# Composite step weights on four row groups, high parts by GpSimd, copies by ScalarE, ahead of a recurrent block

## What is computed

```
x  += cross_attention(x, ctx, mask)          # 16 heads of 8
x  += windowed_attention_with_sinks(x)       # 16 heads of 64, rotary
x  += moe(x)                                 # 8 experts of 512, top 2, and a shared one
x  += attention_lstm(layernorm(x), ctx)      # 32 steps, one after the other
x   = four mamba layers, two halves of the batch
x  += low-rank gated feed-forward(x)
```

## Time and profile before

| what | value |
|---|---|
| three runs | 659.81, 659.59, 658.29 us; median 659.59 |
| profiled execution | 659.47 us, of which the span from first to last instruction is 657.7 us |
| busy share of the span | PE 84%, DVE 72%, ACT 47%, POOL 27% |
| chain of work that ended last | PE 40%, DVE 29%, ACT 13%, issue 11%, POOL 5% |
| prologue of the recurrence | about 200 to 212 us after the span's start |
| recurrence | about 212 to 433 us |

### The profile page before, as it was taken

The page is one execution under the profiler, slowest core; times in us unless marked ns, Lnnn a source line. Parts: engine busy times, 40 slices in busy tenths (PEclk is TensorE's granted clock), DMA queues, the critical chain, the costliest instruction groups (busy, mean ns, idle before and its releaser), DMA issues.

```text
span 657.7 us, 20735 instructions
## 1 busy us (share of the span) xinstructions
PE 553.9 (84%) x8471; PEld 424.7 (65%) x8471; DVE 471.3 (72%) x1834; ACT 306.5 (47%) x902; POOL 179.3 (27%) x217
## 2 busy tenths in 40 slices
PE   6968778669997999999999999966998898889856
PEld 4535543358875888888888888854655665666544
DVE  2978638875345677777777777752898899899883
ACT  3768636226556344434443444335545554555501
POOL 4255629227000000000000000005357346634700
PEclk9979969699995555555555555557988998899887
DMA  9900000010002000000000000000000000000000
GB/s 315 421 8 2 1 5 0 2 47 1 1 5 92 4 4 3 4 4 3 4 4 4 4 3 4 5 2 0 1 0 1 1 1 0 1 1 0 1 0 9
DMA packets 6256, 16.07 MB, mean 24 GB/s; under 512 B 2656, under 2 KB 3432, under 8 KB 5648
## 3 DMA queue, kind: packets, MB, share of 16 engines
q1 hardware_dynamic: 5744, 14.47, 6.0%
q10 hardware_dynamic: 416, 0.26, 0.1%
HBM read 14.60 MB, written 0.13 MB: 22 GB/s over the span
## 4 chain that ended last, share of the span: by engine, by line
PE 40%; DVE 29%; ACT 13%; issue 11%; POOL 5%; DMA 1%; DVEq 0%; ACTq 0%; POOLq 0%
PE bank L1721 8%; PE bank L1627 6%; PE bank L1789 6%; ACT esp L666 3%; PE bank L1557 3%; PE bank L1570 2%; DVE ssum L1168 2%; ACT a L653 2%; ACT e L668 2%; DVE asp L1158 2%; DVE rz L1203 2%; DVE opre L1144 2%; POOL T L438 2%; DVE opre L1147 2%; DVE opre L1145 2%
## 5 line engine op out<-in xcount | busy, mean ns | idle before, releaser
L1627 PE MATMUL bank<-esp,qblk 128*128 128x1 f16 (+1 forms) x2048 | 66.8, 167 | 11.9 <-ACT esp L666 11.9
L474 POOL MEMSET ctxT<- 128x128 f32 x1 | 0.3, 312 | 277.7 <-DVE xres L1210 277.7
L1627 PEld LDWEIGHTS bank<-esp,qblk 128*128 128x128 f16 x2048 | 61.4, 104 | 17.2 <-ACT esp L666 17.2
L1627 PE MATMUL bank<-hsp,kT 128*128 128x2 f16 x2048 | 63.5, 166 | 1.9 <-DVE hsp L1196 1.7
L1627 PEld LDWEIGHTS bank<-hsp,kT 128*128 128x128 f16 x2048 | 59.5, 104 | 2.0 <-issue 1.9
L653 ACT ACTIVATE a<-opre 128x4 f32<-128x4 f32 x64 | 13.1, 205 | 80.8 <-DVE opre L1147 80.8
L1236 DVE SCALAR_TENSOR_TENSOR T<-bank,bct,T 128x256 f32<-128x256 f32 x112 | 46.4, 473 | 2.2 <-PE bank L1802 2.2
L1223 DVE TENSOR_TENSOR_SCAN qblk<-ctxT,bank 128x512 f32<-128x512 f32 x32 | 37.7, 1208 | 5.6 <-PE bank L1789 5.3
L660 ACT ACTIVATE gact<-bank,lgate 128x16 f32<-128x16 f32 x64 | 17.5, 274 | 46.3 <-PE bank L1627 46.3
L1223 DVE TENSOR_TENSOR_SCAN w<-kT,bank 128x512 f32<-128x512 f32 x32 | 37.6, 1205 | 1.1 <-PE bank L1789 1.1
L1627 PEld LDWEIGHTS bank<-asp,lsp 128*128 128x128 f16 x768 | 25.5, 105 | 17.2 <-DVE asp L1158 17.1
(11 more groups left out here) (331 smaller groups left out, 1411.6 us busy)
## 6 DMA issues: line engine op xcount, KB each, us to landing
w<-in_w_dram SPq DMA_DIRECT2D x2, 2048.0 KB
ctxT<-in_ctxT_dram SPq DMA_DIRECT2D x8, 256.0 KB, 6.7
wqkv<-in_qkvT_dram SPq DMA_DIRECT2D x1, 1536.0 KB, 12.2
w<-in_mw_dram SPq DMA_DIRECT2D x1, 1024.0 KB, 4.9
lw<-in_lw_dram SPq DMA_DIRECT2D x1, 960.0 KB, 23.6
rows<-in_rows_dram SPq DMA_DIRECT2D x1, 772.0 KB, 9.9
wqkv<-in_fw_dram SPq DMA_DIRECT2D x1, 532.0 KB, 3.6
T<-in_mask_dram SPq DMA_DIRECT2D x1, 512.0 KB, 5.9
```

The lines of the kernel that those rows point to most:

```text
L1627: return pe.matmul(out, lhsT, rhs, start=start, stop=stop, skip_group_check=True)
```

## The change

The composites of the four layers move to the four row groups of the array: layer l has its two factors on partitions 32l to 32l+7. `dtw` comes in four transfers instead of one. The eight small turns become matmuls with the identity that write 32 rows each (8 useful), so that layer l's rows come out on partitions 32l; ACT copies them in four pieces. In the prologue the composites' matmuls go through the layers for the first chunk and then for the second, and wait first for two gates' outputs on ACT. ACT writes only `gx32`; POOL rounds it to the high part; DVE keeps its three operations on each gate and loses the composites' copies, which ACT takes over after its table load. `l_gxps` and `m_comp` become one semaphore, `l_ps`.

```diff
-        m_dt = maskb[:, :].bitcast(F32)[:, 0:ML * MC * MR]
+        m_dt = maskb[:, :].bitcast(F32)[:, 0:ML * MC * MR + 32]
-        dtw = maskb[0:MR, :].bitcast(F32)[:, 1024:1024 + ML * MI]
-        xpd = wqkv[0:MR, 1856:1856 + ML * MI]
+        dtw = [maskb[32 * l:32 * l + MR, :].bitcast(F32)[:, 1024:1024 + MI] for l in range(ML)]
+        xpd = [wqkv[32 * l:32 * l + MR, 1856:1856 + MI] for l in range(ML)]
...
-            sp.dma_start(dtw, arr["dtw"]).then_inc(sem["d_ssm"], 16)
+            for l in range(ML):
+                sp.dma_start(dtw[l], arr["dtw"][:, l * MI:(l + 1) * MI]).then_inc(sem["d_ssm"], 16)
...
+            for g in range(4):
+                pool.wait_ge(sem["l_gx"], g + 1)
+                pool.tensor_scalar(gx[:, 0:S, 0, g, :], gx32[:, :, g * B:(g + 1) * B], 1.0, 0.0, ALU.mult, ALU.add) \
+                    .then_inc(sem["l_gxhigh"], 1)
...
-            for k in range(2):
-                act.activation(xpd[:, k * 512:(k + 1) * 512], bank[2 + k][0:MR, :], ACT.Copy).then_inc(sem["m_wdt"], 1)
+            for l in range(ML):
+                act.activation(xpd[l], bank[2][32 * l:32 * l + MR, 0:MI], ACT.Copy).then_inc(sem["m_wdt"], 1)
...
-                act.wait_ge(sem["l_gxps"], g + 1)
+                act.wait_ge(sem["l_ps"], g + 1)
-                for to in (gx32[:, 0:1, g * B:(g + 1) * B], gx[:, 0:1, 0, g, :]):
-                    ins = act.activation(to_time(to), share, ACT.Identity, bias=gbias[:, g:g + 1],
-                                         scale=lgx[:, g // 3:g // 3 + 1])
-                ins.then_inc(sem["l_gx"], 1)
+                act.activation(to_time(gx32[:, 0:1, g * B:(g + 1) * B]), share, ACT.Identity, bias=gbias[:, g:g + 1],
+                               scale=lgx[:, g // 3:g // 3 + 1]).then_inc(sem["l_gx"], 1)
             act.preload_act_table_set("exp_and_others")
+            for l in range(ML):
+                act.wait_ge(sem["l_ps"], 4 + l + 1)
+                act.activation(wdt[l], bank[COMP[l]][:, :], ACT.Copy).then_inc(sem["m_wdt"], 1)
...
-                dve.wait_ge(sem["l_gx"], g + 1)
+                dve.wait_ge(sem["l_gxhigh"], g + 1)
...
-                for l in ((), (0,), (1,), (2, 3))[g]:
-                    dve.wait_ge(sem["m_comp"], l + 1)
-                    dve.tensor_copy(wdt[l], bank[COMP[l]][:, :]).then_inc(sem["m_wdt"], 1)
...
-            for n in range(ML * MC):
-                pe.transpose(bank[2 + n // 4][0:MR, n % 4 * P:(n % 4 + 1) * P], m_dt[:, n * MR:(n + 1) * MR], ident)
+            for l in range(ML):
+                for ch in range(MC):
+                    at = (l * MC + ch) * MR
+                    pe.matmul(bank[2][32 * l:32 * l + 32, ch * P:(ch + 1) * P], m_dt[:, at:at + 32], ident, start=True, stop=True)
...
-            for l in range(ML):
-                if COMP[l] == 1:
-                    pe.wait_ge(sem["l_gx"], 2)
-                for ch in range(MC):
-                    ins = pe.matmul(bank[COMP[l]][:, ch * MI:(ch + 1) * MI], xpd[:, l * MI + ch * P:l * MI + (ch + 1) * P],
-                                    dtw[:, l * MI:(l + 1) * MI], start=True, stop=True)
-                ins.then_inc(sem["m_comp"], 1)
+            pe.wait_ge(sem["l_gx"], 2)
+            for ch in range(MC):
+                for l in range(ML):
+                    ins = pe.matmul(bank[COMP[l]][:, ch * MI:(ch + 1) * MI], xpd[l][:, ch * P:(ch + 1) * P], dtw[l],
+                                    start=True, stop=True)
+                    if ch == MC - 1:
+                        ins.then_inc(sem["l_ps"], 1)
```

More of the change, by code:

```diff
@@ L291, in build @@
              "f_gate", "f_sub", "f_exp", "f_cw", "f_cwps", "f_cwT", "f_h", "f_act", "f_y", "f_acc", "f_b2")
-        sems("d_lw", "l_w", "l_stat", "l_max", "l_scale", "l_kv", "l_hi", "l_rest", "l_gxps", "l_gx",
+        sems("d_lw", "l_w", "l_stat", "l_max", "l_scale", "l_kv", "l_hi", "l_rest", "l_ps", "l_gx", "l_gxhigh",
              "l_gxlow", "l_zero", "g_ps", "g_act", "c_new", "c_tanh", "h_hi", "h_lo", "s_hi", "m_c", "m_t", "m_d",
@@ L295, in build @@
              "y_st", "y_tr")
-        sems("d_late", "d_ssm", "m_turns", "m_comp", "m_wdt", "m_setup",
+        sems("d_late", "d_ssm", "m_turns", "m_wdt", "m_setup",
              "m_xt", "m_xp", "m_uz", "m_up", "m_uc", "m_sig", "m_uu", "m_p", "m_bcs", "m_inv",
@@ L374, in _ @@
             sp.wait_ge(sem["x_res"], 1)
-            sp.dma_start(dtw, arr["dtw"]).then_inc(sem["d_ssm"], 16)
+            for l in range(ML):
+                sp.dma_start(dtw[l], arr["dtw"][:, l * MI:(l + 1) * MI]).then_inc(sem["d_ssm"], 16)
             m_proj = arr["mw"][:, ML * 2 * MI:ML * 2 * MI + ML * MC * (6 * MN + MR)].rearrange("p (n k) -> p n k", n=ML * MC)
-            sp.dma_start(m_dt.rearrange("p (n k) -> p n k", n=ML * MC), m_proj[:, :, 6 * MN:]).then_inc(sem["d_ssm"], 16)
+            sp.dma_start(m_dt[:, 0:ML * MC * MR].rearrange("p (n k) -> p n k", n=ML * MC), m_proj[:, :, 6 * MN:]).then_inc(sem["d_ssm"], 16)
             sp.wait_ge(sem["a_o"], NJ)
@@ L384, in _ @@
             sp.dma_start(m_in, arr["mw"][:, 0:ML * 2 * MI]).then_inc(sem["d_late"], 16)
-            sp.wait_ge(sem["l_gxps"], 4)
+            sp.wait_ge(sem["l_ps"], 4)
             sp.dma_start(m_out, arr["mw"][:, ML * 2 * MI + ML * MC * (6 * MN + MR):]).then_inc(sem["d_late"], 16)
@@ L1533, in _ @@
                 a_out(j)
-            pe.wait_ge(sem["d_ssm"], 32)
-            for n in range(ML * MC):
-                pe.transpose(bank[2 + n // 4][0:MR, n % 4 * P:(n % 4 + 1) * P], m_dt[:, n * MR:(n + 1) * MR], ident)
+            pe.wait_ge(sem["d_ssm"], 16 * (ML + 1))
+            for l in range(ML):
+                for ch in range(MC):
+                    at = (l * MC + ch) * MR
+                    pe.matmul(bank[2][32 * l:32 * l + 32, ch * P:(ch + 1) * P], m_dt[:, at:at + 32], ident, start=True, stop=True)
             pe.transpose(bank[4][0:2 * ML * MC, 0:P], v("convb", 0, 2 * ML * MC), ident).then_inc(sem["m_turns"], 1)
@@ L1552, in f_hidden @@
                 if e == 1:
-                    pe.wait_ge(sem["m_wdt"], 3)
+                    pe.wait_ge(sem["m_wdt"], ML + 1)
                 w = w1[:, e * F:(e + 1) * F] if e < E else ws[:, 0:F]
@@ L1615, in _ @@
                 pe.matmul(bank[g][:, 0:TOK], lw[:, g * D:(g + 1) * D], xnT[:, :], start=True, stop=True) \
-                  .then_inc(sem["l_gxps"], 1)
+                  .then_inc(sem["l_ps"], 1)
             pe.wait_ge(sem["l_rest"], 2 * B + 1)
-            for l in range(ML):
-                if COMP[l] == 1:
-                    pe.wait_ge(sem["l_gx"], 2)
-                for ch in range(MC):
-                    ins = pe.matmul(bank[COMP[l]][:, ch * MI:(ch + 1) * MI], xpd[:, l * MI + ch * P:l * MI + (ch + 1) * P],
-                                    dtw[:, l * MI:(l + 1) * MI], start=True, stop=True)
-                ins.then_inc(sem["m_comp"], 1)
+            pe.wait_ge(sem["l_gx"], 2)
[5 more added lines that the diff above has]
+                        ins.then_inc(sem["l_ps"], 1)
             def mm(out, lhsT, rhs, start=False, stop=False):
@@ L1671, in half @@
                 if main == (0, 0):
-                    pe.wait_ge(sem["m_wdt"], 3 + ML)
+                    pe.wait_ge(sem["m_wdt"], 2 * ML + 1)
                 pe.wait_ge(sem["h_hi"], nth(g, t))
```

## The result

The changed kernel takes 655.56 us (median of 8 runs, 654.57 to 657.46) against 659.62 us of the kernel before beside it (8 runs, 658.29 to 660.52): ratio 0.9948, 95% interval 0.9933 to 0.9963. Two later comparisons gave 0.9946 (0.9924 to 0.9968) and 0.9945 (0.9926 to 0.9965). It is 0.5% faster; the forecast was 657.2 us.

A forecast was written before the change was run, and what follows sets the result against it. The prologue's end was taken as bound by PE's composites, with DVE's gate parts just behind. Shortening both starts the recurrence at 208.86 instead of 211.21, 2.35 us earlier: 657.2 us, range 655.6 to 659.2.

The forecast's parts named there:

- Both branches: Prologue's end: PE's composites release the recurrence at 211.21, DVE's gate parts at 210.75; shortening composites alone gives 0.46 us.
- The composites: Prologue on PE: eight matmuls on four row groups take 2.24 us instead of 7.12, ending at 206.4.
- no packing: Rival, prologue on PE: composites still take 7.12 us, no change, 659.6 us; chance 0.09.
- POOL's rounding: Prologue gate parts: POOL rounds each high part in 0.45 us (0.34 to 1.0), so DVE starts at 203.03.
- The block: Prologue gate parts: POOL operations delay DVE's two-input operations 0.35 us each, three times, 1.05 in all (0 to 1.65).
- whole block: Rival, prologue gate parts: POOL blocks DVE fully three times, 1.65 us lost; gain 1.65, 657.9 us; chance 0.15.
- The sum: Prologue's end: recurrence starts at 208.86 instead of 211.21, 2.35 us earlier, giving 657.2 us.
- no block: Rival, prologue gate parts: POOL slips into DVE's pauses; gain 3.4 us, 656.2 us; chance 0.12.
- What was costed at nothing: ACT's composite copies (slack 1.4 us), new turns at the experts' head (1.2 us) and SP's issues stay covered.
- the clock rival: Experts' head: new matmuls keep PE's clock up, 1.5 to 1.8 us more gained, 655.6 us; chance 0.09.
- The median: Whole kernel: 657.2 us, 0.36% faster, taken 0.12 us above the profiled execution less 2.35.

The follow-up runs named there:

- the split: Changed kernel, but only four steps of gates 2 and 3 formed before the recurrence and ACT's table load moved earlier; ratios to the kernel before 0.9924, 0.9954, 0.9941.
- the added memsets: Changed kernel plus a POOL memset of the same size behind each high part, run once for timelines; DVE's gate parts took 5.08 us, as in the changed kernel.

## Why the prediction was right, point by point

- **Both branches had to be shortened**: right, and shown by doing each alone: inner stretches of 9.84 and 9.51 us against 9.52, and 6.52 with both. The estimate that the row groups alone give 0.46 us was not borne out (0.32 more): it left out that the packed form ties all composites to ACT's second gate, and DVE's copies to them.
- **The composites**: forecast 2.24 us for two rounds. At the lower clock the trace has 2.09 with its tail, in seven profiles; in the change's first profile 1.54, because the clock rose meanwhile, and 1.15 in its second at the upper level. Not a bound in either case. The rival "no packing" fell: groups with 8 of 32 partitions in use overlap too.
- **POOL's rounding**: taken as 0.45, measured 0.41, and 0.55 where it met DVE; DVE started at 203.09, forecast 203.03.
- **The block**: this term was mis-sized. 0.35 for each of three POOL operations, 1.05 us in all; measured 0.44. The row behind it lost 1.07 of the 1.20 us that were left of POOL's operation. Here the first pair starts just as far apart, 0.07 us (203.37 and 203.44), and DVE loses 0.20 of the 0.34 left; so the starts are not the reason. That row has 512 columns and a POOL operation with two inputs, here it is 256 columns and one input; whether one of these matters was not tried. The case "whole block" (1.65) fell with it.
- **The sum**: recurrence forecast at 208.86, found at 208.23; gain in the prologue 2.98 instead of 2.35. The block is 0.61 of the difference; DVE started 0.06 later, and PE followed DVE after 0.06 us and not 0.14. The measured gain lies between the forecast and the rival "no block" (3.4).
- **What was costed at nothing** stayed so. ACT was free 1.21 us before it was wanted (forecast 1.4). The new turns took 0.66 us, under the 1.2 taken and under the 1.04 of before; ACT's exponential still waited 1.27 us. L1557's successor took 5.24 us for its 16 records as before, so the clock rival did not occur.
- **The median**: the 2.99 us of the prologue are 0.45%, inside all three intervals. The medians differ by more, 4.06, 3.65 and 3.27 us. The first, 655.56 us, stands at the low end of the stated range, which was put there for a gain by the clock at the experts' head that did not occur. That it falls there is luck.
- **The rest of the 4 us**: of it the prediction says nothing. The stage behind the recurrence took 216.2 to 217.2 us in nine of the fourteen profiles, with and without the change, and 217.9 to 218.6 in five. In the nine the clock was up for a while in the first 12 us, in the five it was not. Among the nine the stage is in the main shorter the earlier the clock rises, as the second 6 us of the stage show, before and in the change (the last three values are the granted clock, the DMA's share and its rate):

```profile
443.80:449.80 6.00, 5.56 (x26) 4.81 (x27) 0.42 (x1) 2.20 (x5) 0.00 (x0) 0.67 0.00 0
440.70:446.70 6.00, 5.35 (x27) 4.70 (x28) 0.42 (x1) 2.40 (x6) 0.00 (x0) 0.73 0.00 0
```

So the 0.9 us between the first two profiles go with the clock (0.67 and 217.2 us, 0.73 and 216.3). That the medians differ by more than the prologue is best put down to the same, which these runs bear out but do not isolate.

Open is why all four profiles with the split lacked that early time at the upper clock level (one of them had a shorter one, after 12 us), and only one of the ten without the split. Nothing in that stage's program differs. The time at which the stage begins does not sort them: with a start 434.3 us into the span one profile has the full early time (the added memsets) and one has not (the split version's second).

## What to carry to other kernels

When two branches end within half a microsecond of each other, a change to one of them looks worthless; cost both from the timelines and shorten them together, and test each alone to know which one paid. Read such a test by a stretch that the clock does not touch: a 0.45 us gain here was the clock's. Small matmuls of few rows belong on different row groups and banks: eight of them went from 7.2 us to 2.1 at the same clock. Where TensorE's clock moves between its levels, a gain of 1 to 2 us in one stage can vanish in the next: follow it by marks through the whole trace before calling the edit good or useless.

## What the runs showed of the hardware

- A POOL operation that reads SBUF held up DVE operations with two SBUF inputs by 0.15 us on average at 256 columns (0.20, 0.20 and 0.07 in the change); memsets by nothing (5.67 against 5.08 us for the same twelve operations). At 512 columns one such meeting cost 1.07 us.
- On four row groups with 8 of 32 partitions in use, and with the four banks taken in turn, matmuls overlap 3.4-fold: 16 records in 2.09 us at 1.2 GHz, 1.15 at 2.4 GHz, against 7.19 on one group at 1.2 GHz.
- In the stage behind the recurrence the clock was at the upper level for some microseconds within its first 12 us in nine profiles and not in five; those five took 217.9 to 218.6 us for the stage instead of 216.2 to 217.2, as much as the split gained ahead of it.
